# Column maxima of the weights by TensorE and VectorE in a two-layer attention and FFN kernel

## The reference

```python
x = x + _L0_xattn_ref(_layernorm(x), ctx_1024, mask_BxS2_ik0, q_w, q_b, k_w, k_b, v_w, v_b)   # 16 heads of 32
x = x + _L0_ffn_ref(_layernorm(x), packed_weight, weight_scale, bias)                       # ternary weights
x = x + _L1_xattn_ref(_layernorm(x), ctx_1024, Wq, bq, Wk, bk, Wv, bv, Wo, bo)               # 16 heads of 64
x = x + _L1_ffn_ref(_layernorm(x), w_freq_real, w_freq_imag, bias)                          # FFT, product, inverse FFT
```

## Time and profile before

| | before |
|---|---|
| median of 3 runs | 1131.73 us (1128.67 to 1133.52) |
| the profiled execution's own time | 1130.68 us |
| its span | 1128.9 us |
| granted TensorE clock, mean | 0.926 of full |
| TensorE busy | 922.6 us (82%) |
| VectorE busy | 811.0 us (72%) |
| ScalarE busy | 670.1 us (59%) |
| GpSimd busy | 566.4 us (50%) |

### The profile page before, as it was taken

One profiled execution on the slowest core, in us unless ns is written; L12 is line 12 of the kernel. 1 busy time (PEld: TensorE's weight loads), 2 busy tenths in 40 slices (PEclk: granted clock), 3 DMA queues, 4 the chain that ended last, 5 costly groups with the idle time before them and its releaser, 6 DMA issues.

```text
span 1128.9 us, 18053 instructions
## 1 busy us (share of the span) xinstructions
PE 922.6 (82%) x6227; PEld 505.6 (45%) x6227; DVE 811.0 (72%) x1417; ACT 670.1 (59%) x1936; POOL 566.4 (50%) x602
## 2 busy tenths in 40 slices
PE   0488976766866998999799789989997996798794
PEld 0345763333423554555455445544554554444441
DVE  6487766457869778978886897789777868725632
ACT  2236773247558677767885776778667757415601
POOL 2303662605247366746764584668466745804504
PEclk9789989787878999999999999999998999799798
DMA  9461484456656656584766757555847555521602
GB/s 282 99 159 26 97 161 85 98 107 148 151 82 114 136 89 109 108 186 84 134 139 136 114 110 176 101 108 108 186 79 127 126 105 97 111 79 33 117 38 74
DMA packets 352474, 130.40 MB, mean 116 GB/s; under 512 B 333439, under 2 KB 342592, under 8 KB 349439
## 3 DMA queue, kind: packets, MB, share of 16 engines
q1 hardware_dynamic: 352383, 129.25, 55.5%
HBM read 33.57 MB, written 15.96 MB: 44 GB/s over the span
## 4 chain that ended last, share of the span: by engine, by line
PE 47%; DVE 17%; ACT 10%; issue 10%; DMA 7%; POOL 6%; SPq 3%; POOLq 0%; ACTq 0%; DVEq 0%
PE wb L188 13%; PE wb L190 13%; PE wb L189 13%; ACT pr L933 5%; PE wb L1470 3%; DMA prT<-ph 3%; DVE xh L1195 2%; SPq L568 2%; DMA xT<-xh 2%; DVE parts L1013 2%; ACT xh L958 2%; DVE ph L1277 2%; POOL xr L795 1%; PE scores L188 1%; POOL pr L769 1%
## 5 line engine op out<-in xcount | busy, mean ns | idle before, releaser
L769 POOL TENSOR_TENSOR pr<-pr,sm 128x616 f32<-128x616 f32 x128 | 174.2, 1361 | 231.6 <-DVE sm L1272 216.2
L933 ACT ACTIVATE pr<-scores,bound,factor 128x77 f32<-128x77 f32 x640 | 255.6, 419 | 8.6 <-ACT bound L927 0.8
L188 PE MATMUL wb<-xT,wq_hl 128*128 128x512 f16 (+1 forms) x400 | 155.7, 389 | 27.8 <-DMA xT<-xh 20.3
L189 PE MATMUL wb<-xT,wq_hl 128*128 128x512 f16 (+1 forms) x400 | 155.4, 389 | 0.0
L190 PE MATMUL wb<-xT,wq_hl 128*128 128x512 f16 (+1 forms) x400 | 155.0, 387 | 0.0
L946 ACT ACTIVATE ph<-pr 128x618 f16<-128x618 f32 x128 | 93.3, 730 | 80.3 <-POOL pr L769 50.8
L933 ACT ACTIVATION_READ_ACCUMULATOR pr<-scores,bound,factor 128x1 f32 x640 | 132.7, 207 | 0.0
L188 PE MATMUL wb<-wo_hl,qc 128*128 128x512 f16 x276 | 105.6, 382 | 8.7 <-DVE x L1211 4.6
L189 PE MATMUL wb<-wo_hl,qc 128*128 128x512 f16 x276 | 105.5, 382 | 0.0
L190 PE MATMUL wb<-wo_hl,qc 128*128 128x512 f16 x276 | 105.4, 382 | 0.0
L1211 DVE SCALAR_TENSOR_TENSOR xr<-wb,factor,xr 128x512 f32<-128x512 f32 x72 | 52.2, 736 | 57.9 <-PE wb L190 57.9
(11 more groups left out here) (212 smaller groups left out, 2443.2 us busy)
## 6 DMA issues: line engine op xcount, KB each, us to landing
xr<-in_x SPq DMA_DIRECT2D x6, 1024.0 KB, 5.9
out_x<-xr SPq DMA_DIRECT2D x6, 1024.0 KB, 5.1
xr<-in_wk SPq DMA_DIRECT2D x3, 1024.0 KB, 6.7
xr<-in_wq SPq DMA_DIRECT2D x3, 1024.0 KB, 10.2
xr<-in_wv SPq DMA_DIRECT2D x3, 1024.0 KB, 6.8
k1b<-scr_k SPq DMA_DIRECT2D x16, 154.0 KB, 5.3
scr_k<-k1b SPq DMA_DIRECT2D x7, 308.0 KB, 7.2
x<-in_x SPq DMA_DIRECT2D x2, 1024.0 KB, 7.1
```

The lines of the kernel that those rows point to most:

```text
L188: pe.matmul(out, lhs(0), rhs(0), start=start, stop=False, **kw)
L189: pe.matmul(out, lhs(0), rhs(1), start=False, stop=False, **kw)
L769: pool.tensor_tensor(v, v, s, ALU.mult).then_inc(probs_ready, 1)
L933: ins = act.activation(pr[U % 3][:, h // 4, cols], sc[:, U % 2, h // 4, cols], ACT.Exp, bias=bound[:, U % 2, h:h + 1], scale=k["factor"][: ...
```

## The change

GpSimd no longer reduces over partitions. `joined_maximum` clamps the column, masks it to powers of two and multiplies the identity matrix (bf16, `identb`) by it, row by row, into a diagonal matrix `diag`. TensorE multiplies a matrix of ones by the diagonal (`spread`), so that each of the 128 partitions holds all 128 values, in the free columns 384 to 511 of a bank of `sc`. `find_scale` reduces them along the free axis on VectorE. A power of two is exact in bf16, and the maximum of the masked values is the masked maximum. The matmul stands at a slot written out by hand for each of the nine tensors. `diag` is one tile, so each maximum waits until the one before it has been multiplied. The identity (64 KB in f32) is loaded first of all and no longer between the ternary weights and the tables, and its cast to bf16 moves to the start.

```diff
@@ find_scale
-    step(dve.tensor_scalar(a, a, 1e-30, 1e37, ALU.max, ALU.min))
-    step(dve.tensor_scalar(a.bitcast(I32), a.bitcast(I32), 0x7F800000, None, ALU.bitwise_and))
+    step(dve.tensor_reduce(a, spread_of(n), AX.X, ALU.max))
...
+        def spread_of(n):
+            return sc[:, n % 2, 0, 384:384 + P]
@@ sync
+            sp.dma_start(ident, a["eye"]).then_inc(eye_in, 16)
             load_weights("CTX", ctx_in, [a["ctxT"][:, 0:2, :], a["ctxT"][:, 2, :], a["ctxT"][:, 3, :]])
...
-            sp.dma_start(ident, a["eye"]).then_inc(tern_in, 16)
@@ gpsimd
-            def all_reduce(name):
-                n = NTH[name]
-                settle()
-                pool.wait_ge(absmax_ready, n + 1)
-                pool.partition_all_reduce(allmax[:, n:n + 1], absmax[:, n:n + 1], P, bass.bass_isa.ReduceOp.absmax).then_inc(allmax_ready, 1)
-                pool.wait_ge(allmax_ready, n + 1)
...
-            all_reduce("CTX")
             clear(mrow[:, :, :])
-            all_reduce("WK0")
-            all_reduce("WV0")
...
@@ vector
             def joined_maximum(name, n):
                 slot = NTH[name]
-                dve.tensor_reduce(absmax[:, slot:slot + 1], parts[:, slot, 0:n], AX.X, ALU.max).then_inc(absmax_ready, 1)
+                a = absmax[:, slot:slot + 1]
+                step(dve.tensor_reduce(a, parts[:, slot, 0:n], AX.X, ALU.max))
+                step(dve.tensor_scalar(a, a, 1e-30, 1e37, ALU.max, ALU.min))
+                step(dve.tensor_scalar(a.bitcast(I32), a.bitcast(I32), 0x7F800000, None, ALU.bitwise_and))
+                if slot >= 1:
+                    dve.wait_ge(allmax_ready, slot)
+                dve.tensor_scalar(diag[:, :], k["identb"][:, :], a, None, ALU.mult).then_inc(absmax_ready, 1)
...
+                dve.wait_ge(eye_in, 16)
+                step(dve.tensor_copy(k["identb"][:, :], ident))
                 maximum("CTX", ctx_in)
@@ tensor
+            def spread(name):
+                n = NTH[name]
+                pe.wait_ge(absmax_ready, n + 1)
+                if n >= 2:
+                    pe.wait_ge(scale_ready, n - 1)
+                pe.matmul(spread_of(n), ones[:, :], diag[:, :], start=True, stop=True, skip_group_check=True).then_inc(allmax_ready, 1)
+
             pe.wait_ge(prep, PREP0)
+            spread("CTX")
+            spread("WK0")
             pe.wait_ge(zeroed, 1)
             for g, (i, s) in enumerate(SLOTS):
+                if (i, s) == (-1, 2):
+                    spread("WV0")
+                if (i, s) == (-1, 5):
+                    spread("WQ0")
+                if (i, s) == (-1, 12):
+                    spread("WF")
+                if (i, s) == (0, 1):
+                    spread("WK1")
+                if (i, s) == (0, 15):
+                    spread("WV1")
+                if (i, s) == (1, 3):
+                    spread("WQ1")
+                if (i, s) == (1, 14):
+                    spread("WO")
```

More of the change, by code:

```diff
@@ L250, in __call__, with find_scale @@
         self.dve.wait_ge(self.sem, v)
-def find_scale(dve, step, k, slot, allmax, allmax_ready, n, top):
+def find_scale(dve, step, k, slot, allmax, allmax_ready, n, top, spread_of):
     dve.wait_ge(allmax_ready, n + 1)
     a = allmax[:, slot:slot + 1]
-    step(dve.tensor_scalar(a, a, 1e-30, 1e37, ALU.max, ALU.min))
-    step(dve.tensor_scalar(a.bitcast(I32), a.bitcast(I32), 0x7F800000, None, ALU.bitwise_and))
+    step(dve.tensor_reduce(a, spread_of(n), AX.X, ALU.max))
     step(dve.reciprocal(k["scale"][:, slot:slot + 1], a))
@@ L302, in layers @@
         scrap = sb("scrap", [P, 1 + 3 * ND], F32)
+        diag = sb("diag", [P, P], BF16)
         absmax, allmax, parts = sb("absmax", [P, 9], F32), sb("allmax", [P, 9], F32), sb("parts", [P, 9, 4], F32)
@@ L327, in layers @@
         keys_cleared, values_cleared = sem("keys_cleared"), sem("values_cleared")
-        vb1_in, zeroed, pool_idle = sem("vb1_in"), sem("zeroed"), sem("pool_idle")
+        vb1_in, zeroed, pool_idle, eye_in = sem("vb1_in"), sem("zeroed"), sem("pool_idle"), sem("eye_in")
         nsin_in, fold_ready, fold_hi, fold_lo = sem("nsin_in"), sem("fold_ready"), sem("fold_hi"), sem("fold_lo")
@@ L827, in _ @@
                     bias_row("WV0", vb0, brow[:, 0:D], F_BV0, 0)
-                    all_reduce("WQ0")
-                    all_reduce("WF")
-                    all_reduce("WK1")
                     first_rows(FIRST_ROWS[1])
@@ L834, in _ @@
                 if (i, s) == (0, 16):
-                    all_reduce("WV1")
                     bias_row("WV1", vb1[0], brow[:, D:2 * D], F_BV1, 1)
@@ L838, in _ @@
                     bias_row("WV1", vb1[1], brow[:, 2 * D:3 * D], F_BV1, 2)
[L839 to L842, removed]
                 for e in groups_at(g):
@@ L1030, in scaling @@
                 slot = NTH[name]
-                find_scale(dve, step, k, slot, allmax, allmax_ready, slot, TOP[name])
+                find_scale(dve, step, k, slot, allmax, allmax_ready, slot, TOP[name], spread_of)
                 s, sc_ctx = k["scale"][:, slot:slot + 1], k["scale"][:, S_CTX:S_CTX + 1]
@@ L1055, in ternary @@
             def ternary():
-                dve.wait_ge(tern_in, 32)
+                dve.wait_ge(tern_in, 16)
                 for s in range(4):
                     step(dve.tensor_scalar(enc[:, s, :], pk, 2 * s, 3, ALU.logical_shift_right, ALU.bitwise_and))
-                step(dve.tensor_copy(k["identb"][:, :], ident))
                 dve.tensor_scalar(ternrow, enc, -1.0, None, ALU.add).then_inc(tern_rows, 1)
```

## The result

| | before | changed |
|---|---|---|
| median | 1131.57 us (4 runs, 1128.67 to 1133.52) | 1086.01 us (4 runs, 1083.82 to 1091.27) |
| profiled execution, its span | 1130.68 us, 1128.9 us | 1083.82 us, 1082.0 us |
| granted TensorE clock, mean | 0.926 | 0.947 |

The ratio is 0.9601, 95% interval 0.9561 to 0.9641: 4.0% faster, by 45.6 us in the medians. The forecast was 1094, so the direction and the range held and the gain came out 7.8 us larger than the 37.8 worked out.

A forecast was written before the change was run, and what follows sets the result against it. GpSimd's library switches, each followed by idle time put down to "issue", were taken to make the weight preparation late. The stages summed to 37.8 us: 1130.68 less 37.8 is 1092.9, and 1.05 for the median gives 1094 us, range 1078 to 1112.

The forecast's parts named there:

- TensorE's wait for WF: Transposes and last value tile behind WF's matmul wait for VectorE some 7 us; the restart at 1.2 GHz costs 1.7 us.
- query projection: Behind WF's scale: starts at 66.0 instead of 77.74, already at the higher clock level, worth -13.4 us at its end.
- VectorE's wait for WK1: TensorE reaches WK1's matmul only behind the first spectrum tile, so VectorE waits 3.8 us, hidden by GpSimd's late first probabilities.
- first probabilities: GpSimd's first probabilities, 7.32 us late at 104.69, would start with their sums: -14.2 us, carried through to 187 us.
- rows behind WV1: GpSimd's bias rows start 10.9 us earlier; VectorE's wait for normalised rows ends at 203.9: -11.1, in all -25.3 us.
- query projection of the second layer (WQ1): Scale gives 1.5 us, ScalarE's wait for probabilities 5.37; of 6.9 us TensorE lets through about 6: -31.3 in all.
- value products (WO): Switch out holds GpSimd until 322.41; TensorE's 6.10 us wait at 332.98 goes, with 0.4 of clock: -37.8 in all.
- signs of being wrong: TensorE wait over 3 us at a diagonal other than WF's, a load now waited for, or over 784 us behind 345.
- (a): Each stage moves only by its scale, the DMA or TensorE's order being next late: -16, or 1115.7 us; chance 0.17.
- (c): Slower: TensorE stands at its seven matmuls inside the loop, 52.5 us against 37.8 gained, or 1146 us; chance 0.04.
- (d): The switches remain because GpSimd's other work loads code again; the added 5.4 us shows alone, 1137 us; chance 0.04.
- (b): All of GpSimd's gaps go in full, 50.4 us, or 1081 us; chance 0.12.

The follow-up runs named there:

- switches back: Changed kernel with GpSimd's operation over partitions put back at its nine places into an unused tile, scales still from TensorE and VectorE; 1124.64 us, ratio to before 0.9921.
- WK1 earlier: Changed kernel with the matmul of WK1's diagonal moved ahead of the first spectrum tile; 1085.15 us, ratio 0.9580.
- change again: The changed kernel itself, unedited, measured beside the kernels with moved bias loads on one chip; 1086.86 us (5 runs), ratio 0.9611.
- WO's switch: Changed kernel with GpSimd's operation over partitions put back for WO alone, into an unread tile, one switch in and one out; 1095.55 us, ratio 0.9673.
- all moves: Changed kernel with WF's diagonal a slot later, WK1's ahead of the first spectrum tile, two bias loads behind the store of keys; 1080.01 us, ratio 0.9540.
- WF later: Changed kernel with the matmul of WF's diagonal moved one slot later, behind the transposes and the last value tile; 1084.83 us, ratio 0.9578.

## Why the prediction was right, and where it was mis-sized

| step | predicted | trace of the change |
|---|---|---|
| first key matmul | -1.9 | 26.77 to 24.79, -2.0 |
| scale of WQ0 | -15.3 | 53.09 to 37.70, -15.4 |
| TensorE's wait for WF | 7 us, restart at 1.2 GHz | 7.79 us, 0.63 us for a 512 wide matmul, granted clock 0.50 from 60 to 63 |
| query projection | at 66.0, worth -13.4 | at 66.45, scores 90.20 to 78.36, -11.8 |
| VectorE's wait for WK1 | 3.8 us | 3.31 us |
| first probabilities | -14.2 | -14.1 |
| rows behind WV1 | -25.3 | -25.0 |
| query projection of the second layer (WQ1) | -31.3 | -32.8 |
| value products (WO) | -37.8 | -42.6 |
| behind | 0 | -4.4 in this execution, scatter |

**The mechanism** was right: GpSimd's gaps went, and "switches back", which returns them without the old scales, takes back 38.6 us. Up to 190 us every step is right to 0.8 us, but for the scores at 78.36. There VectorE waits 4.14 us (66.84) for ScalarE's half of the value tile that ran late and at the lower clock; at the first probabilities the 1.6 us are back. The prediction let GpSimd's old lateness hide VectorE's wait for WK1. "WK1 earlier" shows that in the changed kernel this wait does delay the first probabilities, by 2.6 us, so it was hidden against the kernel before and not free.

**The term that was mis-sized is WO's.** The prediction took "those 6.1 us and 0.4 of clock", 6.5 in all. From the projection of the earlier trace rows (321.63, in the change 289.53, 32.1 us earlier) to the value products (42.6 us earlier) the stage gave 10.5 us, 8.9 in "change again". It is made of four parts. The wait of 6.10 us is the first. The second is the projection ahead of it, which the prediction held at its pace: it took 5.2 us before, at a granted clock of 0.52, and takes 2.6 us in the change, at 1.00. The scores behind the wait and the next projection, at 0.50 before, lost 0.7 and 1.1 us to the clock, where the prediction had 0.4. 6.1 + 2.6 + 0.7 + 1.1 = 10.5 us.

The second part is not a price of the switch itself. In "WO's switch" the projection runs fast with the switch in, and the wait grows to 9.05 us instead of 6.10: what the switch fixes is when the scores can start, 11.9 us after the projection's start there and 11.4 before, and a slow projection only fills a part of that time. The opposite case is "all moves", which has no switch and runs the same projection slowly (the second row is a stretch, its columns as in the earlier trace rows):

```profile
281.39 0.59 PE L188 MATMUL wb<-xT,wq_hl 128*128 128x512 f16 x1 [3.28 <-DMA xT<-xh]
281.30:285.00 3.70, 3.61 (x9) 1.35 (x10) 1.95 (x6) 2.60 (x12) 0.00 (x0) 0.50 0.91 183
```

Its stage takes 16.4 us against the 24.4 before, a gain of 8.0. So the 6.5 was too small at either pace, and some 2.5 us of the 10.5 hang on a clock level that the switch alone does not set. Why the projection got one level or the other stays open.

**WQ1's term** was short too: the prediction let "about 6" of 6.9 us through, for three value tiles at the lower clock as before, and the stage gave 7.1 us up to WO's projection (-25.0 to -32.1), 7.8 up to its own. Between the scores at 247.53 (222.48 in the change) and the first value product at 271.31 (238.66) the clock rose:

```profile
247.50:271.30 23.80, 16.39 (x99) 9.16 (x100) 13.73 (x24) 13.62 (x38) 8.92 (x8) 0.86 0.44 99
222.40:238.60 16.20, 13.03 (x99) 7.54 (x99) 13.06 (x20) 13.65 (x39) 7.34 (x6) 1.00 0.68 151
```

The 99 matmuls of either stretch take 3.4 us less in the change, and TensorE's waits 4.2 us less.

**The rest.** With the stages as they came, 42.6 us, the sum would read 1130.68 - 42.6 = 1088.1, and with the 1.05 us to the median 1089. The two medians of the change were 1086.0 and 1086.9, so of the 7.8 us some 5 are the two terms, and 2 to 3 lie within the scatter of the stretch behind. That stretch is also where the forecast could have been lucky or unlucky by 8.5 us.

**Readings.** The prediction calls 5.86 us "a switch in". That is VectorE's wait for the answer; GpSimd's own idle time ahead of its operation at 193.28 was 7.06 us, and in the first 1.6 us of it the column was not there yet. Of its signs of being wrong, one is met by the letter: TensorE waits over 3 us at two other diagonals, those of CTX (11.08 us) and WK0 (4.09 us, at 15.44). Both stand at the start, and the first key matmul behind them waits another 9.06 us for VectorE's split of the weights, so they cost nothing.

**The rivals.** (a) each stage moves only by its scale, 1115.7, is out by 29 us. (c), TensorE standing at its matmuls: two of the seven in the loop made it wait over 1 us, 7.79 and 1.94 us, the two that the sum had. (d) one switch is left, ahead of 18.27, and nobody waits for it. (b), all gaps in full, 1081, lies 5 us from the result, nearer than the forecast's 1094. But it comes near by two errors against each other: it leaves out WF's wait, which "WF later" shows to cost 4.9 to 5.5 us, and it has 7.1 us for WO, which gave 10.5.

The Trainium skill, GPSIMD Engine Reference, section 4 (When to use GPSIMD), calls GpSimd the only option for a reduction over partitions. The rows speak against it for one column of maxima that may be rounded to powers of two: 0.25 + 0.22 + 0.29 us on VectorE and TensorE, where GpSimd spent 13.0 us with its two switches.

## What to carry to other kernels

Count the price of an operation that needs another library of GpSimd with both switches, in and out, and look for it not where its result is waited for but where GpSimd's next ordinary work is: here putting the operation back, with its result unused, took back 38.6 of 45.6 us. When a wait of TensorE goes, don't take its length as the gain: a slow matmul run ahead of it hides a part of the hold-up. Count from where that run starts to where the work behind the wait can start, and price the matmuls on both sides at both clock levels, for a range. An in-order DMA queue keeps a wait for a slow engine alive for everything behind it, so once the engine is faster, look next at what stands behind its semaphore in that queue (two loads moved by a few places were worth 5 to 6 us at WQ1's maxima and 4.6 at the value products).

## What the runs showed of the hardware

- A switch of GpSimd out of the library of its operation over partitions took 6.7 to 7.6 us of idle time inside the loop, a switch in 5.7 to 7.1 us (in the 7.06 us at 193.28, before, 1.6 us passed until the column was there). The profile puts it down to "issue", or to an engine that had long been done.
- A VectorE instruction of 0.23 us lasted 2.61 us while GpSimd's clearing of a 128x3072 tile ran (2.66 us). The Trainium skill, SBUF — State Buffer, section "SBUF: two separate sides", has GpSimd and some forms of VectorE's instructions share one pair of ports that the first to come holds for its whole instruction; the trace agrees (41.51 + 2.61 = 44.12 against 41.44 + 2.66 = 44.10). So does the kernel before: a product of 8 columns, 0.29 us in the change, took 1.20 us and ended at 97.40, the clearing at 97.38. Not every instruction is held: in the change one of 0.20 us ran at its usual length inside the same clearing.

```profile
94.72 2.66 POOL L803 MEMSET ph<- 128x3072 f16 x1
96.20 1.20 DVE L1038 TENSOR_SCALAR kb<-kb,scale 128x8 f32<-128x8 f32 x1
```

```profile
38.74 2.68 POOL L800 MEMSET ph<- 128x3072 f16 x1
40.72 0.20 DVE L1066 TENSOR_SCALAR factor<-inv 128x1 f32<-128x1 f32 x1
```

- The same projection behind a rest of 3.2 to 3.8 us ran at a granted clock of 0.52 before, 1.00 in the change and in "WO's switch", and 0.50 in "all moves".
- The same steady work of 780 us scattered by 8.5 us between executions; a stretch of 50 us at a granted clock of 0.90 instead of 1.00 is one visible difference, whose cost was not measured.
